# One last fold in one VectorE operation, and a new order of statements on four engines

## The chip, the cores and the metric

The kernel runs on one core of a Trainium2 chip. The metric is the device time of one execution in microseconds (us). Below, "the profile" is one execution recorded by the hardware profiler. Engines: TensorE (PE, its weight loads PEld), VectorE (DVE), ScalarE (ACT), GpSimd (POOL), SyncE (SP).

## The reference, cut to what matters

```
for l in range(2):                                   # L0, a graph network, two layers
    m_left, m_right = h @ W_left[l].T, h @ W_right[l].T
    u = h @ m_left.T / temper   (upper triangle and diagonal), h @ m_right.T / temper   (lower)
    e = exp(u) * adj
    h = relu(layer_norm((e / (sum(e) + 1e-10)) @ (h @ W_lin[l].T + b_lin[l])))
x = layernorm(x + h)
q, k, v = x @ Wq.T, x @ Wk.T, x @ Wv.T + bv           # L1, attention, 12 heads of 32
scores = q @ k.T * scale + (adj + adj)
row_nonzero = any(scores != 0, axis=-1)
p = nan_to_num(softmax(where(row_nonzero, scores, -inf)))
x = layernorm(x + (p @ v) @ Wo.T + bo)
```

There are 128 graphs of 128 nodes with 384 features. A row whose scores are all zero ("dead") must give zero. The kernel decides that from the row's maximum and from the sum of its scores.

## The kernel before, in words

The 128 graphs are worked in 32 groups of four. One *pass* (`body(p)` on each engine) does L0 of group `it` and L1 of group `it - 1`; what L1 does for its last graph (`pv`, `to`, `po` with b = 3) comes at the start of the next pass. Pass 0 (which also rounds the weights, `setup`), pass 1 and the last passes 32 and 33 leave parts out. Products are made from float16 pairs: a high part rounded by ScalarE, a low part (the difference) by VectorE or GpSimd, three matmuls for each product.

Each engine has its own written-out list of statements; they meet through semaphores. TensorE's statements of one pass: `nl(l, c)` six products of layer l with W_left and W_right, nine matmuls of 512 columns each; `hl(l, b)` the linear part of graph b, nine of 384; `u(l, h)` scores of two graphs, 18 of 256; `ctx(l, b)` the context, three of 386; `th(k)` and `x1t(k)` four transposes each; `qk(c)` six, nine matmuls of 512 each; `v(b)` nine of 384; `scores(b, c)` 12 small groups on 32 rows; `pt(b, r)` four transposes of the softmax weights; `pv(b)` 36 matmuls of 33 columns; `to(b)` three transposes of the attention output `o`; `po(b)` nine of 384.

VectorE reads most results out of PSUM: `nl`, `qk`, `pt`, `x1t`, `to` form low parts; `scores(b, j)` subtracts the adjacency and takes the row's extreme (`nmax`); `rs_of(b)` is a reciprocal and a multiplication by the mask `live`; `pv(b)` scales to `o`; `den`, `bn`, `z_variance`, `inv_std(0)`, `norm_z` are the layer norm of L0's first layer, after which TensorE transposes `z` in `th`; `po_stats` and `fin` are the last layer norm. ScalarE does the exponentials (`exps`, `exp_u`), the rounding and `fin`. GpSimd does low parts (`hl`, `v`, `xt`), the masks, powers and the folds.

The eight PSUM banks have a written-out order of use, `BANK_USES`. A stage that gets a bank waits (`await_bank`) until the stage that had it before has been read, by the signal in `READ`.

The dead-row sum: for each graph b, `folds(b)` on GpSimd adds halves of the 12 x 128 scores, 64 + 64, 32 + 32, ... in six folds in the tile `fold`, and a seventh addition writes `total` (12 numbers), signal `s_tot`. VectorE's `live_of(b)` waits for `s_tot` and makes `live`. `scores(b)` for b >= 2 waits for `fold1` of b - 2 before it overwrites `s`.

Of the kernel before, what the change touches and what calls it, by code (L numbers as in the profile page):

```python
# [5 lines left out]
GROUP = 4  # L6
# [24 lines left out]
def program(nc, x, xT, adj, adjT, weights, biases, ln_cols, ln_rows, out):  # L31
# [5 lines left out]
    with ExitStack() as stack:  # L37
# [62 lines left out]
        def signal(name, per_group):  # L100
# [12 lines left out]
            for p in ("u_full", "u_read", "u_sum", "e_raw", "e_ok", "e_hi_ok", "e_lo_ok"))  # L113
# [16 lines left out]
        fold1, fold2, fold3, fold4, fold5, fold6, s_tot = (  # L130
            signal(p, GROUP) for p in ("fold1", "fold2", "fold3", "fold4", "fold5", "fold6", "s_tot"))
# [15 lines left out]
                     s_full, s_ok, s_tot, fold1, fold2, fold3, fold4, fold5, fold6, p_ok, pt_full, pt_hi, pt_lo, pv_full, live_ok, rcp_ok,  # L147
# [9 lines left out]
        def uses(*runs):  # L157
# [29 lines left out]
        class Pass:  # L187
# [40 lines left out]
            def await_bank(self, eng, stage, *parts):  # L228

                last = {}  # L230
# [101 lines left out]
        def _(pool):  # L332
# [148 lines left out]
            def body(p):  # L481
# [3 lines left out]
                hl(p, 0, 1)  # L485
                out_bias(p, 0)
                weigh(p, 0, 0)
                e_rest(p, 0, 0)
                weigh(p, 0, 1)
                hl(p, 0, 2)  # L490
                e_rest(p, 0, 1)
                out_bias(p, 1)
                hl(p, 0, 3)
                out_bias(p, 2)
                y2_power(p, 3)
                scale_adj(p)
                z_power(p, 0)
                out_bias(p, 3)
                v(p, 0)
                folds(p, 0)  # L500
                folds(p, 1)
                v(p, 1)
                xt(p, 0)
# [12 lines left out]
                hl(p, 1, 2)
                hl(p, 1, 3)
                xt(p, 2)
                y2_power(p, 1)
                mask_left(p)  # L520
                mask_right(p)
                y2_power(p, 2)
# [11 lines left out]
        def _(act):  # L534
# [142 lines left out]
            def body(p):  # L677
                nl(p, 0, 0)
                setup(p, 2)
                setup(p, 3)  # L680
                setup(p, 4)
                nl(p, 0, 1)
# [4 lines left out]
                nl(p, 0, 5)  # L687
                x1_norm(p, 2)
                x1_norm(p, 3)
                hl(p, 0, 0)  # L690
# [3 lines left out]
                x1t(p, 1)  # L694
                x1t(p, 2)
                round_e(p, 0, 0)
                exp_u(p, 0, 1)
                fin(p, 2)
                hl(p, 0, 2)
                qk(p, 0)  # L700
                round_e(p, 0, 1)
                hl(p, 0, 3)
                ctx(p, 0, 0)
                qk(p, 1)
                ctx(p, 0, 1)
# [5 lines left out]
                setup(p, 5)  # L711
                qk(p, 5)
                setup(p, 6)
                v(p, 0)
                th(p, 0)
                th(p, 1)
                exps(p, 0, 0)
                exps(p, 0, 1)
                exps(p, 0, 2)
                th(p, 2)  # L720
                exps(p, 0, 3)
                exps(p, 1, 0)
                pt(p, 0, 0)
                exps(p, 1, 1)
# [3 lines left out]
                pt(p, 1, 0)  # L728
                setup(p, 7)
                nl(p, 1, 1)  # L730
                xt(p, 0)
                exps(p, 1, 2)
                nl(p, 1, 2)
                setup(p, 8)
                setup(p, 9)
                v(p, 1)
                fin(p, 3)
                v(p, 2)
                nl(p, 1, 3)
                to(p, 0)  # L740
# [8 lines left out]
                exps(p, 2, 2)  # L749
                hl(p, 1, 0)  # L750
                exps(p, 2, 3)
                pt(p, 2, 0)
                to(p, 1)
                pt(p, 2, 1)
                pt(p, 2, 2)
                exps(p, 3, 0)
                exps(p, 3, 1)
                exps(p, 3, 2)
                exps(p, 3, 3)
                hl(p, 1, 1)  # L760
                v(p, 3)
                fin(p, 0)
                exp_u(p, 1, 0)
                xt(p, 2)
                pt(p, 3, 0)
                round_e(p, 1, 0)
                to(p, 2)
                exp_u(p, 1, 1)
                hl(p, 1, 2)
                round_e(p, 1, 1)  # L770
                pt(p, 3, 1)
                pt(p, 3, 2)
# [17 lines left out]
        def _(dve):  # L790
# [293 lines left out]
            def body(p):  # L1084
# [3 lines left out]
                scale_z(p, 1)  # L1088
                nl(p, 0, 0)
                pv(p, 3)  # L1090
                nl(p, 0, 1)
                scale_z(p, 2)
                scale_z(p, 3)
                inv_std(p, 1)
                to(p, 3)
                shift_z(p, 0)
                shift_z(p, 1)
                shift_z(p, 2)
                shift_z(p, 3)
                nl(p, 0, 2)  # L1100
                resid(p, 0)
                resid(p, 1)
                po(p, 3)
                y_bn(p, 0)
                y_bn(p, 1)
                setup(p, 2)
                setup(p, 3)
                setup(p, 4)
                nl(p, 0, 3)
                resid(p, 2)  # L1110
                resid(p, 3)
                nl(p, 0, 4)
                nl(p, 0, 5)
                y_bn(p, 2)
                y_bn(p, 3)
                y_variance(p)
                hl(p, 0, 0)
                resid_inv(p)
                resid_norm(p, 0)
                hl(p, 0, 1)  # L1120
                resid_norm(p, 1)
                u(p, 0, 0)
                fin(p, 2)
                u_add(p, 0, 0)
# [4 lines left out]
                x1t(p, 2)  # L1129
                hl(p, 0, 2)  # L1130
                hl(p, 0, 3)
                po_stats(p, 3)
                den(p, 0, 0)
                qk(p, 0)
                bn(p, 0, 0)
                bn(p, 0, 1)
                qk(p, 1)
                den(p, 0, 1)
                bn(p, 0, 2)
                bn(p, 0, 3)  # L1140
# [9 lines left out]
                norm_z(p, 3)  # L1150
                qk(p, 5)
                v(p, 0)
                setup(p, 5)
# [4 lines left out]
                th(p, 0)  # L1158
# [3 lines left out]
                th(p, 1)  # L1162
                scores(p, 1, 0)
                th(p, 2)
                scores(p, 1, 1)
                setup(p, 6)
                scores(p, 1, 2)
                pt(p, 0, 0)
                setup(p, 7)
                scores(p, 1, 3)  # L1170
                pt(p, 0, 1)
                pt(p, 0, 2)
                nl(p, 1, 0)
                live_of(p, 0)
# [373 lines left out]
```

## Time and profile before

| | |
|---|---|
| median of 3 runs | 2868.6 us (2867.44 to 2870.93) |
| profiled execution, device time | 2869.89 us |
| its span | 2868.0 us |
| mean granted TensorE clock | 0.992 |
| busy: TensorE | 2794.6 us (97%) |
| busy: VectorE | 2406.5 us (84%) |
| busy: ScalarE | 1770.5 us (62%) |
| busy: GpSimd | 1657.6 us (58%) |

The span goes from the first to the last instruction; the device time has 1.9 us more around it. TensorE is nearly always busy, so what is to be read is where it is not.

### The profile page before, as it was taken

The page shows a single profiled execution, that of the slowest core. Times are in us where ns is not written, and L with a number is a line of the kernel's source. Part 1 is how long each engine was busy: PE and PEld are TensorE (multiplying, and loading weights), DVE is VectorE, ACT ScalarE, POOL GpSimd, SP SyncE. Part 2 cuts the span into 40 slices and gives each one's busy share as a digit, 9 for nine tenths or more (in the row PEclk, how much of TensorE's full clock was granted, in tenths as well). Part 3 has the DMA queues.
Part 4 walks back from the last instruction along what each step waited for, and adds up shares of the span by engine and source line. Part 5 has one row for each costly group of instructions (what it writes and reads, how often), then busy time and mean ns, then how long its engine had stood idle before and what let it go on. Part 6 is the DMA issues. An engine that isn't in the chain of part 4 may idle for free.

```text
span 2868.0 us, 69803 instructions
## 1 busy us (share of the span) xinstructions
PE 2794.6 (97%) x24768; PEld 1790.0 (62%) x24768; DVE 2406.5 (84%) x8042; ACT 1770.5 (62%) x4107; POOL 1657.6 (58%) x2097
## 2 busy tenths in 40 slices
PE   7999999999999999999999999999999999999996
PEld 4566666666665666666666656666666666566664
DVE  5788888888888888888888888888888888888886
ACT  4556666556665556665566655566655666555664
POOL 2556565556565565655565655656555656555554
PEclk9999999999999999999999999999999999999998
DMA  4001011111011010111010110101110101101000
GB/s 151 30 32 45 21 46 40 41 36 34 32 43 43 32 45 21 45 40 44 33 35 31 43 43 31 45 21 45 40 45 32 41 25 43 43 32 45 21 27 21
DMA packets 55976, 112.21 MB, mean 39 GB/s; under 512 B 4944, under 2 KB 37712, under 8 KB 55632
## 3 DMA queue, kind: packets, MB, share of 16 engines
q1 hardware_dynamic: 55632, 107.76, 11.0%
q8 instruction: 199, 3.26, 0.5%
q14 instruction: 145, 1.19, 0.1%
HBM read 82.58 MB, written 25.17 MB: 38 GB/s over the span
## 4 chain that ended last, share of the span: by engine, by line
PE 86%; DVE 10%; ACT 2%; issue 1%; POOL 0%; DMA 0%; DVEq 0%; SPq 0%; POOLq 0%; ACTq 0%
PE psum L1250 62%; PE psum L1260 11%; PE psum L1311 9%; PE psum L1404 3%; PE psum L1378 2%; DVE z L1016 2%; DVE nT_lo L813 2%; DVE pT_lo L811 1%; DVE rs L876 1%; DVE qk_lo L813 1%; ACT qk_hi L536 1%; ACT pT_hi L536 1%; DVE st L915 1%; DVE o L888 1%; DVE y L907 1%
## 5 line engine op out<-in xcount | busy, mean ns | idle before, releaser
L596 ACT ACTIVATE w<-s,nmax 128x128 f32<-128x128 f32 x1536 | 479.4, 403 | 1.9 <-DVE nmax L846 1.9
L1250 PE MATMUL psum<-hT_hi,w_hi 128*128 128x512 f16 x1152 | 439.1, 381 | 13.3 <-POOL hT_lo L379 11.9
L1250 PE MATMUL psum<-hT_lo,w_hi 128*128 128x512 f16 x1152 | 438.7, 381 | 0.0
L1250 PE MATMUL psum<-hT_hi,w_lo 128*128 128x512 f16 x1152 | 438.4, 381 | 0.0
L536 ACT ACTIVATE nT_hi<-psum 128x512 f16<-128x512 f32 x384 | 230.1, 599 | 271.0 <-PE psum L1250 270.9
L463 POOL TENSOR_TENSOR fold<-fold 128x384 f32<-128x384 f32 (+4 forms) x640 | 342.8, 536 | 50.1
L846 DVE CUSTOM_DVE_ANT_0 s<-psum,adj 128x128 f32<-128x128 f32 x1536 | 341.0, 284 | 30.8 <-PE psum L1378 30.0
L463 POOL TENSOR_TENSOR fold<-s 128x768 f32<-128x768 f32 x128 | 242.3, 1893 | 193.5 <-DVE nmax L846 193.5
L387 POOL TENSOR_TENSOR hl_lo<-hl_raw,hl_hi 128x384 fp32r<-128x384 f32 x256 | 245.3, 963 | 147.5 <-ACT hl_hi L536 143.6
L811 DVE TENSOR_TENSOR pT_lo<-psum,pT_hi 128x512 f16<-128x512 f32 x384 | 253.2, 683 | 37.7 <-ACT pT_hi L536 37.5
L536 ACT ACTIVATE pT_hi<-psum 128x512 f16<-128x512 f32 x384 | 222.0, 598 | 85.3 <-PE psum L1260 85.1
L813 DVE SCALAR_TENSOR_TENSOR nT_lo<-psum,nT_hi 128x512 f16<-128x512 f32 x384 | 256.1, 681 | 11.9 <-ACT nT_hi L536 11.7
L430 POOL TENSOR_TENSOR yrstd<-yvar,pw 128x4 f32<-128x4 f32 x32 | 32.4, 1012 | 403.7 <-DVE yvar L996 403.7
L536 ACT ACTIVATE z<-psum,rden 128x384 f32<-128x384 f32 x256 | 138.1, 578 | 182.4 <-DVE rden L962 182.4
L1250 PE MATMUL psum<-w_hi,hT_lo 128*128 128x384 f16 x768 | 250.4, 326 | 0.0
L1250 PE MATMUL psum<-w_lo,hT_hi 128*128 128x384 f16 x768 | 250.4, 326 | 0.0
L1250 PE MATMUL psum<-w_hi,hT_hi 128*128 128x384 f16 x768 | 250.4, 326 | 0.0
L1250 PE MATMUL psum<-xT_hi,w_hi 128*128 128x512 f16 x576 | 219.6, 381 | 0.0
L1250 PE MATMUL psum<-xT_lo,w_hi 128*128 128x512 f16 x576 | 218.7, 380 | 0.0
L1250 PE MATMUL psum<-xT_hi,w_lo 128*128 128x512 f16 x576 | 218.6, 380 | 0.0
L1260 PE MATMUL psum<-ident,w 128*128 128x128 f32 x1536 | 207.4, 275 | 2.6 <-DVE nmax L846 2.2
L1311 PE MATMUL psum<-nT_hi,hT_lo 128*128 128x256 f16 x768 | 209.3, 273 | 0.0
(133 smaller groups left out, 7948.5 us busy)
## 6 DMA issues: line engine op xcount, KB each, us to landing
xTin<-xT SPq DMA_DIRECT2D x32, 768.0 KB, 4.7
xres<-x SPq DMA_DIRECT2D x32, 768.0 KB, 4.6
out<-y SPq DMA_DIRECT2D x128, 192.0 KB, 1.9
adjn<-adj SPq DMA_DIRECT2D x32, 256.0 KB, 4.9
adjT_sb<-adjT SPq DMA_DIRECT2D x32, 256.0 KB, 5.0
adj<-adj SPq DMA_DIRECT2D x32, 256.0 KB, 2.8
x<-weights SPq DMA_DIRECT2D x4, 576.0 KB, 5.4
s<-weights SPq DMA_DIRECT2D x3, 576.0 KB, 6.4
```

The source lines that it names most:

```text
L387: nc.gpsimd.tensor_tensor(hl_lo[:, b, 0:FEAT], hl_raw[:, b], hl_hi[:, b, 0:FEAT].bitcast(f32), ALU.subtract).then_inc(hlr_lo[l].sem, 1)
L463: nc.gpsimd.tensor_tensor(fold[:, :, 0:n], src[:, :, 0:n], src[:, :, n:2 * n], ALU.add)\
L536: return nc.scalar.activation(dst, src, ACT.Copy, scale=scale)
L596: last = nc.scalar.activation(w[:, m], s[b % 2][:, m], ACT.Exp, bias=nmax[b % 2][:, m:m + 1], scale=-1.0)
L811: nc.vector.tensor_tensor(dst, src, rounded, ALU.subtract).then_inc(done.sem, 1)
L813: nc.vector.scalar_tensor_tensor(dst, src, scale, rounded, ALU.mult, ALU.subtract)\
L846: last = nc.vector.tensor_tensor_reduce(out=s[b % 2][:, m], in0=psum[:, SC[j], c * TOK:(c + 1) * TOK], in1=adj2[:, b], scale=-1.0 / TEMPER ...
L1016: nc.vector.tensor_scalar(z[:, b], z[:, b], rstd[0][:, b:b + 1], nmr[:, b:b + 1], ALU.mult, ALU.add)\
L1250: last = mm(dst, a, b, start=(i == 0), stop=(i == total - 1))
L1260: last = transpose(dst[:, n * 128:(n + 1) * 128], src, ident[:])
L1311: last = mm(dst, a, m, start=(i == 0), stop=(i == len(terms) - 1))
L1404: last = mm(dst[:, n * VCOL:(n + 1) * VCOL], a, m, start=(i == 0), stop=(i == 2))
```

## The change

Three things. GpSimd stops after the third fold (16 numbers left for each of 12 heads); `live_of(b)` on VectorE waits for `fold3` and sums the 16 in one `tensor_reduce` into `total`, then makes `live` as before. With that, GpSimd's `folds(b + 1)` waits for VectorE's `s_tot` of b. All four engines' lists of statements stand in another order, and the banks are used in another order. And in `scores` the wait for `qk` of the first graph is merged with the bank's (`also`), so that the later of the two stands. SyncE's statements stay.

```diff
-                for n, src_ok, done in ((TOK // 2, None, fold1), (TOK // 4, fold1, fold2), (TOK // 8, fold2, fold3),
-                                        (TOK // 16, fold3, fold4), (TOK // 32, fold4, fold5),
-                                        (TOK // 64, fold5, fold6)):
+                for n, src_ok, done in ((TOK // 2, None, fold1), (TOK // 4, fold1, fold2), (TOK // 8, fold2, fold3)):
...
-                pool.wait_ge(fold6.sem, p.upto(fold6, b + 1))
-                if b >= 2:
-                    pool.wait_ge(live_ok.sem, p.upto(live_ok, b - 1))
-                elif p.before.l1:
-                    pool.wait_ge(live_ok.sem, p.before.upto(live_ok, b + 3))
-                nc.gpsimd.tensor_tensor(total[b % 2][:], fold[:, :, 0], fold[:, :, 1], ALU.add)\
-                    .then_inc(s_tot.sem, 1)
...
 def live_of(p, b):                                   (VectorE)
+                dve.wait_ge(fold3.sem, p.upto(fold3, b + 1))
+                nc.vector.tensor_reduce(total[b % 2][:], fold[:, :, 0:TOK // 8], AX.X, ALU.add).then_inc(s_tot.sem, 1)
                 dve.wait_ge(s_tot.sem, p.upto(s_tot, b + 1))
...
 def scores(p, b, c):                                 (TensorE)
-                    p.await_bank(pe, "s", *range(TILES * b, TILES * (b + 1)))
-                if b == 0:
+                    p.await_bank(pe, "s", *range(TILES * b, TILES * (b + 1)), also=(("qk", 1),) if b == 0 else ())
+                elif b == 0:
                     pe.wait_ge(qkr_lo.sem, p.upto(qkr_lo, 2 * c + 2))
```

TensorE's order, before and after, from the middle of a pass on (`s` is all three blocks of `scores`):

```
before: qk0 qk1 ctx0,0 ctx0,1 qk2 ctx0,2 ctx0,3 qk3 qk4 qk5 v0 th0 s0 th1 v1 v2 v3 th2 s1 pt0,0 pt0,1 nl1,0 nl1,1 pt0,2 pt1,0 nl1,2 pv0 nl1,3 s2 to0 nl1,4 pt1,1 pt1,2 po0 nl1,5 pv1 hl1,0 s3 to1 hl1,1 pt2,0 pt2,1 pt2,2 u1,0 po1 pv2 u1,1 pt3,0 to2 hl1,2 pt3,1 hl1,3 pt3,2 po2 ctx1,0..3
after:  qk0 ctx0,0 ctx0,1 qk1 ctx0,2 ctx0,3 qk2 qk3 qk4 qk5 th0 th1 v0 s0(0,1) th2 s0(2) v1 v2 v3 s1 pt0,0 pt0,1 nl1,0 pt0,2 nl1,1 pv0 nl1,2 s2 to0 nl1,3 pt1,0 pt1,1 pt1,2 nl1,4 po0 nl1,5 pv1 pt2,0 s3 hl1,0 pt2,1 u1,0 hl1,1 pt2,2 hl1,2 pt3,0 to1 pt3,1 pv2 u1,1 pt3,2 hl1,3 to2 po1 po2 ctx1,0..3
```

VectorE's order around the two places that the prediction speaks of:

```
before: ... den0,1 bn bn z_variance0 qk2 qk3 qk4 fin3 inv_std0 norm_z(4) qk5 v0 scores0 th0 ...
after:  ... den0,1 bn bn bn z_variance0 qk1 qk2 fin3 inv_std0 norm_z(4) qk3 qk4 qk5 th0 v0 th1 scores0 ...
before: ... scores1,1 scores1,2 pt0,0 scores1,3 pt0,1 pt0,2 nl1,0 live0 pt1,0 rs0 nl1,1 pv0 nl1,2 scores2 ... nl1,3 po0 po_stats0 nl1,4 nl1,5 live1 rs1 pv1 hl1,0 scores3 to1 ...
after:  ... scores1,1 pt0,0..2 scores1,2 live0 rs0 scores1,3 pv0 nl1,0 nl1,1 scores2,0..2 to0 scores2,3 nl1,2 pt1,0..2 live1 po0 nl1,3 nl1,4 po_stats0 rs1 nl1,5 pt2,0 pv1 hl1,0 scores3,0..2 u1,0 scores3,3 live2 hl1,1 pt2,1 pt2,2 u_add1,0 to1 rs2 ...
end, before: ... po2 live3 den1,0 po_stats2 den1,1 bn(4) fin1;  after: ... po1 pt3,2 po2 po_stats1 den1,0 po_stats2 den1,1 bn(4) fin1
start, before: ... resid0 resid1 po3 y_bn0 ...;  after: ... resid0 resid1 y_bn0 y_bn1 scale_z3 nl0,3..5 po3 ...
```

GpSimd: `z_power(0)` and `scale_adj` now come ahead of `y2_power(3)` and of two of the four `out_bias`; `v`, `xt` come earlier, the two `folds` of graphs 2 and 3 after them. ScalarE: `th(2)` ahead of all `exps`, `fin(3)` ahead of `pt(0,0)`, and in pass 0 the weight roundings 5 and 6 ahead of `ctx(0,0)`.

## Rows read from the trace of the kernel before

**Rows 1.** Stretches: one steady pass, and the last 88 us (busy time, number of instructions).

```profile
core 0: us, PE busy (x) PEld busy (x) DVE busy (x) ACT busy (x) POOL busy (x), PEclk, DMA share, GB/s
...
1087.52:1175.10 87.58, 86.73 (x775) 55.76 (x774) 74.78 (x252) 54.84 (x129) 51.77 (x65) 1.00 0.12 38
...
2780.00:2868.00 88.00, 59.74 (x584) 37.38 (x582) 60.97 (x224) 41.86 (x100) 37.19 (x53) 0.82 0.06 22
```

**Rows 2.** TensorE's waits from 120 to 2690 us: total, times, longest.

```profile
PE psum L1260 <- DVE o L888: 16.3, 28, 0.6
PE psum L1260 <- DVE z L1016: 7.2, 29, 0.3
```

**Rows 3.** TensorE's timeline around `to(0)`, `to(1)`, `th(0)`: start, us, operation, [idle before].

```profile
1096.17 0.23 PE L1378 MATMUL psum<-qk_hi,qk_lo 32*128 32x128 f16 x4
1096.33 0.55 PE L1260 MATMUL psum<-ident,o 128*128 128x128 f32 x3
...
1105.86 0.22 PE L1378 MATMUL psum<-qk_hi,qk_lo 32*128 32x128 f16 x4
1106.68 0.55 PE L1260 MATMUL psum<-ident,o 128*128 128x128 f32 x3 [0.60 <-DVE o L888]
...
1164.87 0.33 PE L1250 MATMUL psum<-w_hi,xT_lo 128*128 128x384 f16 x1
1165.44 0.66 PE L1260 MATMUL psum<-ident,z 128*128 128x128 f32 x4 [0.25 <-DVE z L1016]
```

**Rows 4.** The chain of waits where the transposes of `x1` start, passes 1 and 31.

```profile
95.48 1.31 PE psum L1260 x12
...
2721.96 1.31 PE psum L1260 x12
```

**Rows 5.** VectorE's timeline: `rs_of(1)`, the last `nmax` of graph 3, L0's layer norm.

```profile
1104.92 1.04 DVE L876 SCALAR_TENSOR_TENSOR rs<-live,rs 128x12 f32<-128x12 f32 x1
...
1109.54 0.08 DVE L846 DVE_READ_ACCUMULATOR2_ANT nmax<- 128x1 f32 x1
...
1158.00 0.15 DVE L959 TENSOR_SCALAR eps_den<-psum 128x2 f32<-128x2 f32 x1
1158.18 0.17 DVE L962 RECIPROCAL rden<-eps_den 128x2 f32<-128x2 f32 x1
...
1160.40 0.17 DVE L986 TENSOR_SCALAR var<-mv 128x4 f32<-128x4 f32 x1
...
1162.45 0.69 DVE L813 SCALAR_TENSOR_TENSOR qk_lo<-psum,qk_hi 128x512 f16<-128x512 f32 x1 [0.69 <-ACT qk_hi L536]
...
1163.74 1.65 DVE L1016 TENSOR_SCALAR z<-z,rstd,nmr 128x384 f32<-128x384 f32 x4
```

**Rows 6.** GpSimd's timeline at the same places.

```profile
1104.78 1.15 POOL L379 TENSOR_TENSOR hT_lo<-xTin,hT_hi 128x512 f16<-128x512 f32 x1
...
1109.76 1.81 POOL L463 TENSOR_TENSOR fold<-s 128x768 f32<-128x768 f32 x1 [0.52 <-DVE nmax L846]
...
1156.94 0.62 POOL L445 TENSOR_SCALAR adj<-adj 128x512 f32<-128x512 f32 x1
1160.66 1.02 POOL L430 TENSOR_TENSOR sd<-var,pw 128x4 f32<-128x4 f32 x1 [3.10 <-DVE var L986]
```

**Rows 7.** The chain of waits: `pt`, `scores`, `nl`, `hl`, `u` on TensorE, start to start.

```profile
1084.11 0.44 PE psum L1260 x4
1084.54 0.61 PE psum L1378 x36
...
1093.83 1.95 PE psum L1250 x9
...
1107.23 1.46 PE psum L1250 x9
...
1110.00 1.96 PE psum L1311 x18
```

**Rows 8.** GpSimd's groups: the first and the last of the four operations removed.

```profile
L463 POOL TENSOR_TENSOR fold<-fold 128x96 f32<-128x96 f32 x128 | 50.0, 391 | 10.0
...
L471 POOL TENSOR_TENSOR total<-fold 128x12 f32<-128x12 f32 x128 | 27.4, 214 | 10.1
```

More of the change, by code:

```diff
@@ L129, in program @@
         s_full, s_ok, p_ok = (signal(p, GROUP * TILES) for p in ("s_full", "s_ok", "p_ok"))
-        fold1, fold2, fold3, fold4, fold5, fold6, s_tot = (
-            signal(p, GROUP) for p in ("fold1", "fold2", "fold3", "fold4", "fold5", "fold6", "s_tot"))
+        fold1, fold2, fold3, s_tot = (signal(p, GROUP) for p in ("fold1", "fold2", "fold3", "s_tot"))
         pt_full, pt_hi, pt_lo = (signal(f"pt_{p}", GROUP * KB) for p in ("full", "hi", "lo"))
@@ L226, in await_apart, with await_bank @@
                 eng.wait_ge(sig.sem, value)
-            def await_bank(self, eng, stage, *parts):
-                last = {}
+            def await_bank(self, eng, stage, *parts, also=()):
+                last = {name: (self.group(READ[name]), i) for name, i in also}
                 for i in parts:
@@ L485, in body @@
                 hl(p, 0, 1)
-                out_bias(p, 0)
[L487 to L491, printed above, removed]
+                weigh(p, 0, 0)
+                weigh(p, 0, 1)
+                e_rest(p, 0, 0)
+                e_rest(p, 0, 1)
+                hl(p, 0, 2)
+                hl(p, 0, 3)
+                out_bias(p, 0)
                 out_bias(p, 1)
-                hl(p, 0, 3)
-                out_bias(p, 2)
-                y2_power(p, 3)
                 scale_adj(p)
                 z_power(p, 0)
+                y2_power(p, 3)
+                v(p, 0)
+                out_bias(p, 2)
                 out_bias(p, 3)
-                v(p, 0)
                 folds(p, 0)
@@ L727, in body @@
                 nl(p, 1, 0)
-                pt(p, 1, 0)
-                setup(p, 7)
+                exps(p, 1, 0)
                 nl(p, 1, 1)
-                xt(p, 0)
+                exps(p, 1, 1)
                 exps(p, 1, 2)
[L733 to L740, printed above, removed]
                 exps(p, 1, 3)
                 xt(p, 1)
+                to(p, 0)
+                xt(p, 2)
+                v(p, 1)
+                setup(p, 8)
+                v(p, 2)
+                nl(p, 1, 2)
+                v(p, 3)
+                setup(p, 9)
+                pt(p, 1, 0)
+                nl(p, 1, 3)
                 pt(p, 1, 1)
@@ L1087, in body @@
                 scale_z(p, 0)
-                scale_z(p, 1)
                 nl(p, 0, 0)
                 pv(p, 3)
+                scale_z(p, 1)
                 nl(p, 0, 1)
+                inv_std(p, 1)
                 scale_z(p, 2)
-                scale_z(p, 3)
[L1094 to L1097, printed above, removed]
+                to(p, 3)
+                nl(p, 0, 2)
+                shift_z(p, 0)
+                setup(p, 2)
+                shift_z(p, 1)
+                resid(p, 0)
+                resid(p, 1)
+                y_bn(p, 0)
+                setup(p, 3)
+                y_bn(p, 1)
+                scale_z(p, 3)
+                nl(p, 0, 3)
+                nl(p, 0, 4)
+                nl(p, 0, 5)
+                setup(p, 4)
+                po(p, 3)
                 shift_z(p, 2)
                 shift_z(p, 3)
[L1100 to L1109, printed above, removed]
                 resid(p, 2)
                 resid(p, 3)
-                nl(p, 0, 4)
-                nl(p, 0, 5)
                 y_bn(p, 2)
@@ L1116, in body @@
                 y_variance(p)
+                u(p, 0, 0)
                 hl(p, 0, 0)
                 resid_inv(p)
+                u_add(p, 0, 0)
                 resid_norm(p, 0)
+                resid_norm(p, 1)
                 hl(p, 0, 1)
[L1121 to L1124, printed above, removed]
                 u(p, 0, 1)
@@ L1129, in body @@
                 x1t(p, 2)
+                fin(p, 2)
                 hl(p, 0, 2)
                 hl(p, 0, 3)
-                po_stats(p, 3)
                 den(p, 0, 0)
                 qk(p, 0)
+                po_stats(p, 3)
                 bn(p, 0, 0)
+                den(p, 0, 1)
                 bn(p, 0, 1)
-                qk(p, 1)
-                den(p, 0, 1)
                 bn(p, 0, 2)
@@ L1150, in body @@
                 norm_z(p, 3)
+                setup(p, 5)
+                qk(p, 3)
+                qk(p, 4)
                 qk(p, 5)
+                setup(p, 6)
+                th(p, 0)
                 v(p, 0)
-                setup(p, 5)
+                th(p, 1)
                 scores(p, 0, 0)
@@ L1161, in body @@
                 v(p, 3)
-                th(p, 1)
+                th(p, 2)
                 scores(p, 1, 0)
-                th(p, 2)
                 scores(p, 1, 1)
-                setup(p, 6)
-                scores(p, 1, 2)
                 pt(p, 0, 0)
-                setup(p, 7)
-                scores(p, 1, 3)
                 pt(p, 0, 1)
                 pt(p, 0, 2)
+                scores(p, 1, 2)
+                live_of(p, 0)
+                setup(p, 7)
+                rs_of(p, 0)
+                scores(p, 1, 3)
+                pv(p, 0)
                 nl(p, 1, 0)
-                live_of(p, 0)
-                pt(p, 1, 0)
-                rs_of(p, 0)
                 nl(p, 1, 1)
-                pv(p, 0)
-                nl(p, 1, 2)
+                setup(p, 8)
                 scores(p, 2, 0)
                 scores(p, 2, 1)
+                scores(p, 2, 2)
                 to(p, 0)
-                setup(p, 8)
-                scores(p, 2, 2)
                 scores(p, 2, 3)
+                nl(p, 1, 2)
+                pt(p, 1, 0)
                 pt(p, 1, 1)
                 pt(p, 1, 2)
+                live_of(p, 1)
+                po(p, 0)
                 nl(p, 1, 3)
-                po(p, 0)
+                nl(p, 1, 4)
                 po_stats(p, 0)
-                nl(p, 1, 4)
+                rs_of(p, 1)
                 nl(p, 1, 5)
-                live_of(p, 1)
-                rs_of(p, 1)
+                pt(p, 2, 0)
                 pv(p, 1)
-                setup(p, 9)
                 hl(p, 1, 0)
@@ L1200, in body @@
                 scores(p, 3, 2)
+                u(p, 1, 0)
+                setup(p, 9)
                 scores(p, 3, 3)
-                to(p, 1)
+                live_of(p, 2)
                 hl(p, 1, 1)
-                pt(p, 2, 0)
                 pt(p, 2, 1)
                 pt(p, 2, 2)
-                u(p, 1, 0)
-                po(p, 1)
                 u_add(p, 1, 0)
+                to(p, 1)
+                rs_of(p, 2)
                 fin(p, 0)
-                live_of(p, 2)
-                rs_of(p, 2)
+                hl(p, 1, 2)
                 pv(p, 2)
-                po_stats(p, 1)
+                live_of(p, 3)
                 u(p, 1, 1)
                 u_add(p, 1, 1)
-                to(p, 2)
-                hl(p, 1, 2)
                 pt(p, 3, 0)
                 hl(p, 1, 3)
+                to(p, 2)
                 pt(p, 3, 1)
+                po(p, 1)
                 pt(p, 3, 2)
                 po(p, 2)
-                live_of(p, 3)
+                po_stats(p, 1)
                 den(p, 1, 0)
@@ L1479, in body @@
                 to(p, 0)
[L1480 removed]
+                nl(p, 1, 3)
+                pt(p, 1, 0)
                 pt(p, 1, 1)
                 pt(p, 1, 2)
+                nl(p, 1, 4)
                 po(p, 0)
```

139 lines of the change are left out of this document (67 added, 72 removed).

## The prediction

> **What bounds the kernel now.** I read the stretches first, then TensorE's waits, then the chain of waits, then the timelines of the two places that they name. One steady pass takes 87.58 us and TensorE is busy for 86.73 of them [rows 1]. So a schedule can give back 0.85 us of a pass, about 1%, unless it makes the matmuls themselves cheaper, and this change alters none. The other engines have room: VectorE 12.8 us, ScalarE 32.7, GpSimd 35.8 in the same pass. They matter only where TensorE waits for them. Between 120 and 2690 us only two waits of TensorE are left [rows 2]: `to(p, 1)`, the transpose of `o`, 28 times, 16.3 us, and `th(p, 0)`, the transpose of the normalised `z`, 29 times, 7.2 us. Together 23.5 us in 29 passes, 0.81 each.
>
> Idle time is a little less than what is lost, since the last matmul's record runs on after the next could have started. From start to start [rows 3]: before `to(0)`, which does not wait, the last scores matmul and the transpose are 0.16 us apart (1096.17, 1096.33); before `to(1)` 0.82 us (1105.86, 1106.68). Lost: 0.66 us. Before `th(0)` 0.57 us (1164.87, 1165.44), where matmuls of this width follow at 0.16: 0.41 us. The true loss is 1.07 us a pass.
>
> How often: the transposes of `x1` start at 95.48 us in pass 1 and at 2721.96 us in pass 31 [rows 4], 2626.5 us in 30 steps, 87.55 each. With pass 31's second half that is 31 passes.
>
> **Why the two waits exist.** `to(1)`: `pv(1)` ends on TensorE, VectorE forms `rs` and `o`, and TensorE has only `hl(1,0)` and `scores(3)` in between, 1.46 + 0.76 us. The second operation of `rs_of` took 1.04 us instead of 0.17 (the row at 1104.92), and ended when GpSimd's `xt` of 1104.78 to 1105.93 ended [rows 5, 6]. So the two engines block each other there. `th(0)`: from the end of `ctx(0,3)` VectorE works through `den` (1158.00), `bn`, `z_variance` (ends at 1160.57, 2.6 us later), then three `qk` subtractions, of which the last waits 0.69 us for ScalarE, and only then the normalisation, 1.65 us, from 1163.74 to 1165.39 [rows 5]. TensorE reaches `th(0)` after three `qk` and one `v`, 3 x 1.95 + 1.46 = 7.3 us [rows 7], just too early.
>
> **The change, part by part.** *Fold.* GpSimd loses four operations for each of four graphs, each 0.21 to 0.39 us [rows 8]: 0.9 to 1.6 us a graph, 3.4 to 6.3 us a pass, from an engine that idles 35.8. Nothing on TensorE waited for it directly: 0. VectorE gains one `tensor_reduce` of 192 numbers into 12. The trace has none. Below, it costs what a tiny operation does, 0.17 us (the reciprocal at 1158.18); above, what reading 512 numbers does, 0.69 us (1162.45) [rows 5]. Its width of 192 puts it a third of the way: I take 0.35. Four times that, plus a hand-over of 0.03 us each (1158.15 to 1158.18), is 1.5 us a pass (0.8 to 2.9). VectorE has 12.8 us free and it lies under TensorE's work: 0, if no consumer stands close behind. Where the cover is gone it costs its own 0.35 us, once for each such place.
>
> *`to(1)`.* TensorE now does `pt(2,0)`, `scores(3)`, `hl(1,0)`, `pt(2,1)`, `u(1,0)`, `hl(1,1)`, `pt(2,2)`, `hl(1,2)`, `pt(3,0)` between `pv(1)` and `to(1)`: 4 x 0.44 + 0.76 + 3 x 1.46 + 1.96 = 8.9 us [rows 7]. VectorE needs `rs_of` 0.35 (1.2 if blocked), `nl`, `pt`, `pv`, together 2.1 to 3 us. The wait goes: -0.66.
>
> *`th(0)`.* From the end of `ctx(0,3)`: `den`, two copies of `z`, the last `bn`, `z_variance` to 2.5 us; GpSimd's power 1.02 [rows 6], and now `y2_power(3)` behind it, at most as much again, since `fin(3)` stands before `inv_std` on VectorE; 4.7 us at worst; `inv_std` 0.5; normalisation 1.65: 6.9 us. `qk(3)` and `qk(4)` are now behind it. TensorE arrives after four `qk`, 7.8 us. Slack 0.9: -0.41.
>
> *What it adds on TensorE.* `th(2)` is now put between the second and third block of `scores(0)`. A turn from transposes to the 32-row matmuls or back costs about 0.1 us more than a step without a turn (0.16 at 1096.17 to 1096.33, against 0.07, which is 0.61 us over the nine steps of four matmuls in `scores`) [rows 3, 7]. One split adds two turns: +0.2, bounds 0 and 0.4.
>
> *What is late next.* I laid every engine's statements end to end from these prices and looked at each bank and each operand. The tightest places are: `scores(2,0)` needs its bank read by `scores(1,3)`, now behind `rs_of(0)`, which waits for `pv(0)`: 0.35 + 0.64 + 0.1 = 1.1 us against TensorE's `nl(1,2)`, 1.95: slack 0.85. `to(0)`: 1.7 us against 2.7: 1.0. `pv(1)` uses the bank that `nl(1,3)` leaves; from the end of `po(0)`, VectorE reads both in 1.15, TensorE has `nl(1,5)`, 1.95: 0.8. `u(1,0)` uses the bank of `pv(1)`; from its end TensorE has two `pt`, `scores(3)` and `hl(1,0)`, 3.1, VectorE `rs_of`, `nl`, `pt`, `pv`, 2.2: 0.9. `to(2)`, `po(1)`, `po(2)` now stand in a row: ScalarE 0.5 and VectorE 0.55 against 1.46: 0.4. `ctx(1,2)` uses the bank of `po(2)`, two contexts after it, six matmuls at 0.16 to 0.18, against one read of 0.55: 0.5. None is negative, so 0 for each; they are thin.
>
> *The hold on `fold`.* `folds(b+1)` now waits for VectorE's `live_of(b)`. For b = 1 the fold of graph 2 starts some 3 us after its scores are ready. `scores(b)` on VectorE waits for the first fold of graph b-2 only: 0. The queue of SyncE: its statements stay, and the load of `adj2` stands behind `store(2)`, hence behind `fin(2)`, which keeps its place between `x1t` and `hl(0,2)`. `scale_adj`, which found its data ready (no idle time at 1156.94), comes an `out_bias` and a power earlier, 1.6 us. Even if it waited all of that, `z_power(0)` behind it idles 3.10 us for VectorE [rows 6]: 0.
>
> *Head and tail.* Pass 0 keeps its serial chain; two weight roundings of ScalarE come ahead of the first `ctx` copies: +0.5, bounds -1 and +2. In the last 88 us TensorE is busy for 59.7 [rows 1]: here the chain of single operations sets the time. `po_stats(1)` is later, `po(3)` behind two more statistics: +1.5, bounds -3 and +5.
>
> **The sum.** 31 x (-0.66 - 0.41 + 0.2) = -27.0; head and tail +2.0; -25.0. The profiled execution took 2869.9 us (span 2868.0, and 1.9 around it), 1.3 above the median of the runs, so 2844.9 in its terms and 2843.6 in the median's: 2844.
>
> **The rivals.**
> *A (0.62)*: as summed, 2834 to 2850. The low end is a split that costs nothing (31 x 1.07 = 33) and a tail that gains 1.5.
> *B, thin slots (0.18)*: one or two of the slots of 0.4 to 0.9 us fail in part. A blocked VectorE operation is late by up to 0.9 us (1.04 against 0.17); `rs_of(1)` now falls into the last folds of graph 2, say. If one such hits a slot of 0.4, TensorE waits 0.5: 31 x (0.87 - 0.5) = 11 us gain, 2859 with the tail. Range 2850 to 2863.
> *C, no difference (0.09)*: what the two waits hid comes back at two slots, 0.7 to 1.0 us a pass: 2863 to 2874. For it: my slots are sums of ten prices and each could be off by that much; against it: all would have to err to one side, and each leaves 0.4 or more.
> *D, the lock race, slower (0.11)*: the reduce's signal releases two things at once: VectorE's own `live` operation and GpSimd's first fold of the next graph, 1.81 us [rows 6]. If the fold goes first, `live` is blocked as `rs` was at 1104.92, and VectorE stands still for 1.8 us, for b = 1 and b = 2, where the scores are already there. Then `nl(1,3)` frees its bank 1.75 late with a slack of 0.8: wait 0.95; and `pt(2,2)`/`hl(1,1)` are late by 1.75 with slacks of 1.2: wait 0.6. Net -0.87 + 1.55 = +0.68 a pass, +21 us: 2891. With one place alone it is +0.1 a pass, rival C. It decides from a stall of about 1.4 us on. Against it: VectorE follows its own signal by 0.03 us, while GpSimd started 0.14 us after `nmax` (1109.62, 1109.76) [rows 5, 6].
>
> The Trainium skill, "SBUF — State Buffer", section on practical consequences, says that a VectorE instruction with two SBUF inputs and a GpSimd instruction that reads SBUF block each other fully and that the first to issue wins; the 1.04 us row agrees. It also says that `tensor_reduce` never contends on this chip, which no run here shows yet. By this rule only `live` and `rs` are exposed, not the reduce. That is the mechanism of D.
>
> **The numbers.** A and B are faster: 0.80. C: 0.09. D: 0.11. A measurement of this kernel tells about 0.2% (5.7 us) from no change. The range that keeps 8 in 10: 2834 to 2864, A and B with their bounds.
>
> **What the changed profile would show.** Right: a steady pass of 86.7 us; the waits for `o` and `z` gone from TensorE's list between 120 and 2690 us; no new row there above 5 us; `total` on VectorE at 0.3 to 0.4 us; `live` with a median near 0.16 us. Wrong: `live` with a median of a microsecond (D); a new wait of TensorE for `oT_lo`, `nmax` or `nT_lo` (B, C); a tail longer than 93 us. I am wrong above all if a slot that I give 0.4 to 0.9 us is in truth shut.

## The result and the profile after

The changed kernel takes 2845.7 us (median of 4 runs, 2845.1 to 2847.13); the kernel before, beside it, 2868.0. Ratio 0.9921 with a 95% interval of 0.9904 to 0.9938: 22 us or 0.8% faster. The forecast was 2844 us, with a range of 2834 to 2864.

The steady pass of the changed kernel, and its last 85 us, by stretches. They answer to [rows 1]:

```profile
1051.27:1137.92 86.65, 86.65 (x777) 55.85 (x775) 76.18 (x256) 55.42 (x128) 46.75 (x50) 1.00 0.11 38
...
2759.00:2844.20 85.20, 55.18 (x549) 35.40 (x546) 58.29 (x223) 38.58 (x91) 28.26 (x31) 0.80 0.06 20
```

A pass takes 86.65 us and TensorE is busy in all of it. VectorE works 1.4 us more, GpSimd 5.0 us less. From 120 to 2690 us the list of TensorE's waits is empty; where [rows 2] had 23.5 us there is no line. The list of its weight loads has only these (total, times, longest). No idle time of the matmuls goes with them, which alone does not prove that they cost nothing (see e8):

```profile
PEld psum L1371 <- issue: 41.3, 148, 0.4
PEld psum L1243 <- issue: 14.5, 88, 0.2
PEld psum L1243 <- DVE oT_lo L802: 4.7, 30, 0.2
PEld psum L1253 <- DVE pT_lo L802: 0.4, 1, 0.4
```

The chain of waits, at the transposes of `x1` in passes 1 and 31 (compare [rows 4]):

```profile
98.14 1.50 PE psum L1253 x12
...
2697.57 1.31 PE psum L1253 x12
```

2599.4 us in 30 passes, 86.65 each, against 87.55: 0.90 us less. Up to the first of the two the new kernel is 1.2 us slower (2.66 us later, of which 1.46 are `hl(0,2)`, which now comes ahead of `x1t`). The 30 passes give -27.0. From the second to the end, with the same correction, it is 2.05 us slower. 1.2 - 27.0 + 2.05 is -23.8 us, the difference of the two spans (2868.0 and 2844.2).

The two operations of `live_of`, from the tiles `total` and `live` of the changed kernel (min/median/max in ns):

```profile
L855 DVE TENSOR_REDUCE total<-fold x128: 333/343/349, 129.0 to 2826.0; 128x12 f32<-128x192 f32 x128
L857 DVE SCALAR_TENSOR_TENSOR live<-nmax,total x128: 170/171/173, 129.4 to 2826.4; 128x12 f32<-128x12 f32 x128
```

### The profile page after: what moved, and what is told of

Read it like the earlier page. It is cut to its first block, busy times and chain, and to the rows that moved or that the text cites. A ratio compares the mean times of both kernels' runs of the same rounds, so it can differ in the third digit from the quotient of the medians.

```text
span 2844.2 us, 69230 instructions
## 1 busy us (share of the span) xinstructions
PE 2792.3 (98%) x24768; PEld 1793.3 (63%) x24768; DVE 2447.5 (86%) x8170; ACT 1784.8 (63%) x4107; POOL 1497.1 (53%) x1585
## 4 chain that ended last, share of the span: by engine, by line
PE 97%; DVE 1%; issue 1%; ACT 1%; DMA 0%; POOL 0%; SPq 0%; POOLq 0%; DVEq 0%; ACTq 0%
PE psum L1243 70%; PE psum L1253 11%; PE psum L1304 9%; PE psum L1397 4%; PE psum L1371 3%; DMA xTin<-xT 0%; DMA s<-weights 0%; ACT w L587 0%; ACT w_hi L527 0%; DVE st L962 0%; POOL hl_lo L387 0%; DVE w_lo L785 0%; DVE st L908 0%; POOL e L416 0%; DVE y L900 0%
## 5 line engine op out<-in xcount | busy, mean ns | idle before, releaser
L461 POOL TENSOR_TENSOR fold<-s 128x768 f32<-128x768 f32 x128 | 232.7, 1818 | 224.5 <-DVE nmax L837 139.6
L527 ACT ACTIVATE hl_hi<-hl_raw 128x384 fp32r<-128x384 f32 x256 | 133.1, 520 | 300.5 <-DVE hl_raw L817 300.5
L387 POOL TENSOR_TENSOR hl_lo<-hl_raw,hl_hi 128x384 fp32r<-128x384 f32 x256 | 252.6, 993 | 125.7 <-ACT hl_hi L527 125.6
L395 POOL TENSOR_TENSOR v_lo<-v_raw,v_hi 128x384 f16<-128x384 f32 x128 | 112.5, 890 | 283.1 <-ACT v_hi L527 283.1
L461 POOL TENSOR_TENSOR fold<-fold 128x384 f32<-128x384 f32 (+1 forms) x256 | 217.8, 851 | 20.0
L1253 PE MATMUL psum<-ident,w 128*128 128x128 f32 x1536 | 220.1, 277 | 4.0 <-DVE nmax L837 2.0
```

Source lines behind the costliest of these rows:

```text
L387: nc.gpsimd.tensor_tensor(hl_lo[:, b, 0:FEAT], hl_raw[:, b], hl_hi[:, b, 0:FEAT].bitcast(f32), ALU.subtract).then_inc(hlr_lo[l].sem, 1)
L395: nc.gpsimd.tensor_tensor(v_lo[:, b, :, 0:HEAD], v_raw[:, b].rearrange("p (h d) -> p h d", h=HEADS), v_hi[:, b, :, 0:HEAD], ALU.subtract). ...
L527: return nc.scalar.activation(dst, src, ACT.Copy, scale=scale)
L1253: last = transpose(dst[:, n * 128:(n + 1) * 128], src, ident[:])
```

## The experiments

Each run was timed beside the kernel before. "A pass" is the distance between the transposes of `x1` in pass 1 and pass 31 divided by 30; it is 87.55 us in the kernel before.

| run | median us | ratio to before, 95% interval | a pass, us |
|---|---|---|---|
| e1 fold only | 2970.4 | 1.0354 (1.0340 to 1.0369) | 90.61 |
| e2 order only | 2845.2 | 0.9919 (0.9905 to 0.9932) | 86.61 |
| e3 `norm_z` first | 2878.2 | 1.0033 (1.0020 to 1.0045) | 87.82 |
| e4 `to(1)` later | 2868.2 | 0.9999 (0.9990 to 1.0008) | 87.51 |
| e5 e3 and `out_bias(3)` later | 2855.7 | 0.9954 (0.9941 to 0.9966) | 87.10 |
| e6 e4 and two banks exchanged | 2850.4 | 0.9936 (0.9924 to 0.9949) | 86.92 |
| e7 e5 and e6 together | 2834.7 | 0.9881 (0.9866 to 0.9896) | 86.43 |
| e8 changed, `th(2)` whole | 2843.9 | 0.9913 (0.9900 to 0.9927) | 86.57 |
| e9 e1 with a tile of its own | 2862.9 | 0.9979 (0.9970 to 0.9988) | 87.29 |
| e10 changed, three reduces | 2866.6 | 0.9994 (0.9985 to 1.0003) | 87.25 |
| e11 changed, `out_bias` early | 2863.1 | 0.9981 (0.9973 to 0.9990) | 87.20 |
| e12 changed, five reduces | 2874.2 | 1.0018 (1.0009 to 1.0027) | 87.44 |

### Which part brings the gain: the fold alone (e1), the order alone (e2)

e1 is the kernel before with the three edits of the fold (signals, `folds`, `live_of`) and no other line changed.

> The order of before, with the fold's change alone. My theory (the order brings the gain, the fold gives none by itself): in the old order the reduce stands in live_of(1), right ahead of rs_of(1), pv(1) and to(1), where TensorE already waits, so its 0.34 us and a hand-over come on top of the wait, unless GpSimd's shorter folds take away the blocked rs operation (1.04 instead of 0.17 us). I expect 2868 + 31 x 0.38 = 2880 us, and at least 2863. Rival (the fold is the gain): 2845 to 2855 us, with TensorE's waits for o and z smaller.

e2 is the changed kernel with the old `folds` and `live_of`:

```diff
-                for n, src_ok, done in ((TOK // 2, None, fold1), (TOK // 4, fold1, fold2), (TOK // 8, fold2, fold3)):
+                for n, src_ok, done in ((TOK // 2, None, fold1), (TOK // 4, fold1, fold2), (TOK // 8, fold2, fold3),
+                                        (TOK // 16, fold3, fold4), (TOK // 32, fold4, fold5),
+                                        (TOK // 64, fold5, fold6)):
...
-                nc.vector.tensor_reduce(total[b % 2][:], fold[:, :, 0:TOK // 8], AX.X, ALU.add).then_inc(s_tot.sem, 1)
```

> The order and banks of after, with GpSimd doing all seven additions as before. My theory: 2843 to 2850 us, TensorE without waits in the middle, VectorE 48 us less busy than in after; in the new order live_of(0) comes 0.4 us after the old, longer folds would be done, so at most 0.3 us a pass is lost there. Rival (the new order works only because GpSimd has 6 us less to do): a new wait behind live_of, 2855 to 2870 us.

e2 took 2845.2 us: the order and the banks are the whole gain, the fold adds nothing to it. e1 took 2970.4 us. The sign was right and the size wrong by eight times: 102 us lost, not 12. e2's time lies in its forecast. The waits of GpSimd in e1, from 120 to 2690 us:

```profile
POOL fold L460 <- DVE total L854: 488.4, 87, 6.6
POOL yrstd L429 <- DVE yvar L988: 347.7, 28, 12.6
```

In the old order `live_of` stands late on VectorE, which cost nothing as long as GpSimd did not need it. Now GpSimd's next fold waits for it, 5.6 us at a time, and with the fold everything queued behind it: `hl`, `weigh`, `e_rest`. And the fold that starts on VectorE's signal blocks an operation on two SBUF tiles that VectorE issues just behind it. VectorE's timeline in e1, and GpSimd's below it:

```profile
1047.81 0.17 DVE L856 SCALAR_TENSOR_TENSOR live<-nmax,total 128x12 f32<-128x12 f32 x1
...
1048.16 1.53 DVE L868 SCALAR_TENSOR_TENSOR rs<-live,rs 128x12 f32<-128x12 f32 x1
...
1047.86 1.80 POOL L460 TENSOR_TENSOR fold<-s 128x768 f32<-128x768 f32 x1 [5.72 <-DVE total L854]
```

`live` is issued 0.05 us before the fold and passes; `rs`, behind it, ends at 1049.69, just after the fold (1049.66). This is the rule in e1, not the exception; the 128 second operations of `rs_of` (min/median/max in ns) in e1, and below in e9, the next run:

```profile
L868 DVE SCALAR_TENSOR_TENSOR rs<-live,rs x128: 170/941/1544, 131.0 to 2957.1; 128x12 f32<-128x12 f32 x128
...
L874 DVE SCALAR_TENSOR_TENSOR rs<-live,rs x128: 170/172/875, 132.0 to 2850.5; 128x12 f32<-128x12 f32 x128
```

### What of e1's loss is the hold (e9)

The third fold writes a small tile of its own, `last`, two of them in turn, so GpSimd's next fold no longer waits for VectorE's sum:

```diff
+        last = [sb(f"last{i}", [HEADS, TOK // 8]) for i in range(2)]
...
                 if b > 0:
-                    pool.wait_ge(s_tot.sem, p.upto(s_tot, b))
+                    pool.wait_ge(fold3.sem, p.upto(fold3, b))
...
+                    if done is fold3 and b > 1:
+                        pool.wait_ge(s_tot.sem, p.upto(s_tot, b - 1))
...
+                nc.vector.tensor_reduce(total[b % 2][:], last[b % 2][:, :, 0:TOK // 8], AX.X, ALU.add).then_inc(s_tot.sem, 1)
```

> The fold's change alone in the order of before, as in the first run, but the third fold writes a small tile of its own, two of them in turn, so that GpSimd's next fold waits for its own third fold and no longer for VectorE's reduce. Theory (the hold on the tile cost the 102 us: GpSimd waited 488 us for total there, and hl_lo and weigh behind it came late): the time falls from 2970 us to 2868 + 31 x 0.38 = 2880 us, 2865 to 2890. Rival (the reduce, and rs blocked by GpSimd's folds, cost it): it stays above 2930 us.

2862.9 us: with the hold go all 102 us of the loss and 5.4 more, so the fold's change by itself is a gain even in the old order, where I had expected a loss (2880, at least 2865). The 107 us between e1 and e9 have two parts that this run takes away together, GpSimd's wait for `total` and most of the blocking of `rs`; how they share it was not tested. In its trace the idle time for `o` is down to this:

```profile
PE psum L1258 <- DVE z L1014: 7.2, 29, 0.2
PE psum L1258 <- DVE o L886: 0.5, 2, 0.2
```

GpSimd is earlier and no longer in the middle of an operation when `rs_of(1)` comes: in the pass read, its `xt` ends at 1015.16, and `rs` starts at 1016.00 and takes 0.17 us. That this is why the wait shrinks was not tested by itself. And it is not gone: from start to start, in the mean of 25 passes, the step before `to(1)` is 0.44 us shorter than in the kernel before, not 0.66, and `pt(3,0)` and `to(2)` take 0.24 us more than there, with next to no idle time in the list for either.

### The wait for `z` alone (e3, e5)

```diff
                 qk(p, 2)
-                qk(p, 3)
-                qk(p, 4)
                 fin(p, 3)
                 inv_std(p, 0)
                 norm_z(p, 0)
...
                 norm_z(p, 3)
+                qk(p, 3)
+                qk(p, 4)
                 qk(p, 5)
```

> The order of before with one move on VectorE: fin(3), inv_std(0) and the four norm_z ahead of qk(3) and qk(4). My theory: the wait for z is a matter of this place alone and is worth 0.41 us a pass: 2868 - 31 x 0.41 = 2855 us, if qk(3), qk(4) and qk(5), now later, still come in time for scores(0); TensorE's wait for o stays. Rival: the wait moves on to the scores or to th(1), 2866 to 2870 us.

It was 10 us slower. TensorE's wait for `z` is gone from the list, and in its place stand 9.7 us of waiting for `qk_lo` (29 times). VectorE's and GpSimd's timelines in e3:

```profile
1077.35 0.96 DVE L1003 TENSOR_SCALAR sd_eps<-sd 128x4 f32<-128x4 f32 x1 [0.48 <-POOL sd L430]
...
1077.28 1.00 POOL L405 TENSOR_TENSOR x<-x,bias 128x384 f32<-128x384 f32 x1
```

`sd_eps` now comes right after GpSimd's power, and so does GpSimd's next statement, `out_bias(3)`, 0.07 us earlier. It takes 0.96 us for a four-column operation. It has one SBUF input, so it is not only operations with two that are blocked. e5 adds one exchange on GpSimd:

```diff
                 z_power(p, 0)
-                out_bias(p, 3)
                 v(p, 0)
+                out_bias(p, 3)
```

> The third run's move (fin(3), inv_std(0), norm_z ahead of qk(3) and qk(4) on VectorE) and, with it, GpSimd's out_bias(3) behind v(0) instead of right behind z_power(0). Theory: in the third run VectorE's first operation after the power, sd_eps, was blocked by out_bias(3) for 0.97 instead of 0.17 us in every pass; with GpSimd idle there it is not, and the time falls by 31 x 0.8 = 25 us from 2878 us to about 2855 us. Rival: the late qk subtractions are the cause (TensorE waits for qk_lo), the blocked operation is not, 2872 to 2880 us.

2855.7 us, with `sd_eps` never above 0.171 us and the wait for `qk_lo` gone as well. The wait for `z` is worth 0.45 us a pass (forecast 0.41), but it needs two engines' orders, not one. The changed kernel has both edits.

### The wait for `o` alone (e4, e6)

TensorE's list (VectorE's likewise):

```diff
                 scores(p, 3, 2)
-                to(p, 1)
                 hl(p, 1, 1)
+                to(p, 1)
```

> The order of before with to(1) moved behind hl(1,1) on TensorE and on VectorE. My theory: 1.46 us of matmuls now cover the 0.66 us that are lost: 2868 - 31 x 0.66 = 2847.5 us, TensorE's wait for o gone, its wait for z as before. Rival: VectorE's chain is the bound there and TensorE waits for pt(2,*) or po(1) instead, 2860 to 2870 us.

No change at all. TensorE's timeline in e4:

```profile
1017.16 0.22 PE L1378 MATMUL psum<-qk_hi,qk_lo 32*128 32x128 f16 x4
1017.99 0.34 PE L1250 MATMUL psum<-w_hi,hT_hi 128*128 128x384 f16 x1 [0.60 <-DVE o L888]
```

`hl(1,1)` now has the very wait that `to(1)` had. It does not read `o`; it writes into the bank out of which VectorE forms `o`. The old order had two reasons to wait at the same place, and the profile names only the first that comes. e6:

```diff
-            ... ("nl1", 4), ("to", 1), ("pv", 2), ("c1", 0)),
+            ... ("nl1", 4), ("hl1", 1), ("pv", 2), ("c1", 0)),
...
-                 ("po", 0), ("pv", 1), ("hl1", 1), ("po", 1), ("pt", 10)),
+                 ("po", 0), ("pv", 1), ("to", 1), ("po", 1), ("pt", 10)),
```

> The fourth run's move (to(1) behind hl(1,1)) and, with it, their two PSUM banks exchanged: hl(1,1) takes the bank that nl(1,4) leaves, to(1) the one that pv(1) leaves. Theory: in the fourth run hl(1,1) waited for the same VectorE operation as to(1) had, because its bank is the one out of which o is formed; with another bank the 0.66 us a pass are covered by its 1.46 us: 2868.5 - 31 x 0.66 = 2848 us, TensorE's wait for o gone. Rival: VectorE's chain behind it (pt, u, po) is as late, 2860 to 2869 us.

2850.4 us, 0.63 us a pass (forecast 0.66). So this half of the gain comes from the new `BANK_USES` as much as from the new order.

### Both, and nothing else (e7)

> The two runs above in one kernel: order of before, four local edits, no change of the fold. Theory: the two waits are independent, 2868.5 - 31 x 1.07 = 2835 us, TensorE without waits in the middle, less than the new order's 2845.7 since scores(0) is not split and head and tail are those of before. Rival: removing one lets the other grow, 2845 to 2855 us.

2834.7 us: the waits add up, 1.12 us a pass (0.45 and 0.63 alone), and this kernel, the one before with four local edits, beats the changed one by 11 us. Its pass takes 86.43 us:

```profile
1000.00:1086.43 86.43, 86.43 (x776) 55.98 (x775) 74.87 (x252) 55.01 (x129) 52.18 (x66) 1.00 0.11 38
```

Between the two spans (2833.5 and 2844.2) lie 10.7 us: 6.4 in the 30 passes, 2.8 ahead of the first of them and 1.5 behind the last, with `hl(0,2)` counted as above.

### The split of `scores(0)` (e8)

```diff
                 scores(p, 0, 1)
-                th(p, 2)
                 scores(p, 0, 2)
+                th(p, 2)
                 v(p, 1)
```

> The changed kernel with th(2) behind scores(0,2) instead of between scores(0,1) and scores(0,2) on TensorE. Theory: two turns between transposes and 32-row matmuls fall away, 0.2 us a pass: 2845.7 - 6 = 2839.5 us, a steady pass of 86.45 us. Rival: the turns cost nothing or th(2) is then late for nl(1,0), 2845 to 2847 us.

The chain of waits, from the first block of `scores(0)` to the end of `v(3)`, first in the changed kernel:

```profile
1070.20 0.45 PE psum L1371 x24
1070.64 0.59 PE psum L1253 x4
1071.23 0.28 PE psum L1371 x12
1071.51 4.49 PE psum L1243 x27
```

and in e8:

```profile
1069.58 0.61 PE psum L1371 x36
1070.19 0.59 PE psum L1253 x4
1070.78 4.39 PE psum L1243 x27
```

5.81 against 5.59 us: the two turns cost 0.22 us, as estimated. But the pass is only 0.08 us shorter and the kernel 1.8 us faster, between the forecast and its rival. The rest shows in the chain: `pv(0)` takes 0.99 us instead of 0.90, and `nl(1,0)` and `pt(0,2)` ahead of it 0.02 more each, 0.13 in all. TensorE has no idle time there. But the list of its weight loads, from 120 to 2690 us, has three waits that the changed kernel's has not:

```profile
PEld psum L1397 <- issue: 11.7, 30, 0.4
PEld psum L1243 <- DVE hT_lo L1030: 10.1, 30, 0.3
PEld psum L1253 <- DVE nmax L837: 9.1, 30, 0.3
```

`hT_lo` is what VectorE makes of `th`, so the rival (`th(2)` late for `nl(1,0)`) came in part. That these waits cause the 0.13 us fits by place and was not tested.

### How wide the slots are (e10, e12, e11)

e10 and e12 put two and four more reduces ahead of the real one:

```diff
+                for i in range(2):
+                    nc.vector.tensor_reduce(spare_out[i][:], fold[:, :, 0:TOK // 8], AX.X, ALU.add).then_inc(spare, 1)
                 nc.vector.tensor_reduce(total[b % 2][:], fold[:, :, 0:TOK // 8], AX.X, ALU.add).then_inc(s_tot.sem, 1)
```

> The changed kernel with the reduce done three times (twice into unused tiles, ahead of the real one), +0.55 to 0.7 us on VectorE for each graph. Theory (slots of 0.8 us behind live_of(1), 1.1 behind live_of(2), 0.4 left at po(2) behind live_of(3)): the slots take it, 0 to 0.2 us a pass, 2846 to 2852 us. Rival (the slots are nearly shut): 31 x 4 x 0.6, up to 2920 us, with new waits of TensorE.

> As the run with three reduces, with five, +1.1 to 1.4 us on VectorE for each graph, 4.4 to 5.6 us a pass. Theory: now the slots are overrun: about 0.5 us at pv(1), 0.2 at pv(2) and pt(3,0), 0.5 at po(2), together 0.5 to 1.2 us a pass: 2861 to 2883 us. Rival (VectorE has 12 us free, it is hidden): 2846 to 2850 us.

e10 took 2866.6 us, more than the theory had and much less than the rival: 0.60 us a pass. TensorE waits at one place only, `po(2)`. VectorE in e10, then GpSimd, then TensorE:

```profile
1028.93 0.60 DVE L858 TENSOR_REDUCE spare_out<-fold 128x12 f32<-128x192 f32 x2
...
1030.63 0.95 DVE L946 TENSOR_TENSOR e<-uLR 128x256 f32<-128x256 f32 x1
...
1032.56 0.54 DVE L804 TENSOR_TENSOR oT_lo<-psum,oT_hi 128x384 f16<-128x384 f32 x1
...
1030.57 0.73 POOL L428 TENSOR_TENSOR e_lo<-e,e_hi 128x256 fp32r<-128x256 f32 x1 [1.68 <-ACT e_hi L529]
...
1033.16 0.34 PE L1247 MATMUL psum<-w_hi,oT_hi 128*128 128x384 f16 x1 [0.54 <-DVE oT_lo L804]
```

The two reduces before `live_of(3)` cost 0.52 us. They push `u_add(1,1)` behind the start of GpSimd's `e_rest`, and it takes 0.95 instead of 0.43 us. In the changed kernel it gets ahead:

```profile
1108.87 0.43 DVE L942 TENSOR_TENSOR e<-uLR 128x256 f32<-128x256 f32 x1
...
1109.32 0.73 POOL L426 TENSOR_TENSOR e_lo<-e,e_hi 128x256 fp32r<-128x256 f32 x1 [1.75 <-ACT e_hi L527]
...
1110.78 0.56 DVE L802 TENSOR_TENSOR oT_lo<-psum,oT_hi 128x384 f16<-128x384 f32 x1 [0.35 <-ACT oT_hi L527]
...
1111.46 0.33 PE L1243 MATMUL psum<-w_hi,oT_hi 128*128 128x384 f16 x1
```

Here `oT_lo` ends at 1111.34, 0.12 us before `po(2)` starts, not 0.4. e12, with twice the load, lost 0.80 us a pass, inside its forecast. TensorE's idle time does not show where: from 120 to 2670 us it is 6.0 us, in 29 passes that lost 23. The steps from start to start do. In the mean of 25 passes, against the changed kernel, `po(1)` and `po(2)` take 0.36 us more, `hl(1,2)` 0.19, `nl(1,2)` 0.12, and the `pt` of graphs 2 and 3 together 0.13. The chain of waits behind `hl(1,2)`, in the changed kernel and then in e12:

```profile
1017.23 1.20 PE psum L1253 x11
...
1025.86 0.03 issue
1025.89 1.42 PE psum L1257 x11
```

So with 1 us more in front of each `live` several slots are overrun, each by less than the load.

e11 exchanges GpSimd's `v(0)` with `out_bias(2)` and `out_bias(3)` in the changed kernel.

> The changed kernel with out_bias(2) and out_bias(3) of GpSimd ahead of v(0) again, right behind z_power(0) and y2_power(3). Theory: they block sd_eps and the nmr behind it, as out_bias(3) did in the third run, 0.8 us each; the slot in front of th(0) is 0.9 to 1.3 us, so TensorE waits 0.3 to 0.7 us a pass: 2855 to 2868 us, sd_eps with a median above 0.7 us. Rival: the blocked operations fit into the slot, 2845 to 2848 us, with the same sd_eps.

2863.1 us, as forecast, 0.55 us a pass. The operations blocked were others than I had named. `sd_eps` passed between the two biases; those hit are the two with two inputs, in `fin(3)` and in `inv_std(0)`. VectorE's timeline in e11, and the row of GpSimd's two biases below it:

```profile
1073.24 0.95 DVE L923 SCALAR_TENSOR_TENSOR nmr<-mv,rstd 128x1 f32<-128x1 f32 x1 [0.47 <-POOL rstd L430]
1074.12 0.16 DVE L996 TENSOR_SCALAR sd_eps<-sd 128x4 f32<-128x4 f32 x1
...
1074.52 0.63 DVE L1001 SCALAR_TENSOR_TENSOR nmr<-mv,rstd 128x4 f32<-128x4 f32 x1
...
1073.18 1.95 POOL L405 TENSOR_TENSOR x<-x,bias 128x384 f32<-128x384 f32 x2
```

Without the biases both take 0.16 us. Where two statements of GpSimd stand is worth 17 us.

## Why the prediction was right, point by point

**What bounds the kernel.** Right. Loss counted from start to start, 1.07 us a pass, not the 0.81 us of idle time: e7 shows that 1.12 us can be had.

**`to(1)`, -0.66.** Right in size, incomplete in cause. The prediction named only the operand `o`. e4 and e6 show a second wait on the same operation, for the bank. I counted a gain for the new place of `to(1)`; it needed the new banks too, and these were in the change.

**`th(0)`, -0.41.** Right in size (0.45 in e5; the prediction counted up to the first transpose, and the four of `th(0)` are 0.06 us shorter in e5 as well). In the changed kernel `z` is ready at 1066.70 and `th(0)` starts at 1067.70: slack 1.0 us, forecast 0.9. The `fin(3)` in front of `inv_std` waits 0.47 us for its power, as expected. What the prediction left out is why GpSimd's biases moved: e3 and e11 show that they would have taken the slot.

**The fold.** The reduce costs 0.343 us; I took 0.35. Its effect on the time was put at 0 and is 0 in the new order (e2: 2845.2 against 2845.7). The prediction's part on the hold was right for the new order (there GpSimd waits for `total` 77 us from 120 to 2690, and TensorE waits for nothing) but would have been wrong by some 100 us for the old one (e1, e9). Cover was a matter of the order, not of the operation.

**The split, +0.2.** The turns cost 0.22 us (e8). With the 1.12 us that the two waits give back (e7) this makes -0.90 a pass, which is what was measured; the forecast was -0.87. Undoing the split in the new order gives back only 0.08 us a pass.

**What is late next.** No slot was overrun. `po(2)` was named as the tightest, at 0.4 us; it has 0.12. Two reduces more ahead of each `live` are enough to overrun it, by 0.60 us a pass (e10).

**Head and tail, +2.0.** Mis-sized: 1.2 us at the head and, with the last pass's gain of 0.9 taken out, 2.9 at the tail, 4.1 together. The passes made good 0.9 of the 2.1 us: 31 x 0.90 is 27.9 instead of 27.0. What in the head and the tail cost it was not tested.

**The rivals.** B and C did not come. D, the lock race, did not come either: the longest `live` of 128 took 0.173 us. It goes 0.05 us before the fold (1102.15 and 1102.20 in VectorE's and GpSimd's timelines), as the prediction argued. Its mechanism is real one operation later: in the old order `rs` stands there (e1). In the new order `rs_of` is never directly behind `live_of(1)` or `live_of(2)`; its second operation is still blocked in 63 of 128 cases by other work of GpSimd (0.96 us instead of 0.17 at worst), but TensorE waits for none of them. Nor is `live` safe everywhere: in e1, 30 of its 128 take 1.2 us, those of graph 3. The Trainium skill's rule, "SBUF — State Buffer", practical consequences, that the first to issue wins for the whole instruction, agrees with these rows. Its statement that `tensor_reduce` never contends agrees too. In the changed kernel no reduce begins while GpSimd is in an operation, so that kernel is no test. In e1 31 do, and in e9 61, and none of them takes over 0.345 us. VectorE in e1, and GpSimd's row below it (two operations, the second from about 1068.3 to 1069.2):

```profile
1068.78 0.34 DVE L854 TENSOR_REDUCE total<-fold 128x12 f32<-128x192 f32 x1
1069.15 1.18 DVE L856 SCALAR_TENSOR_TENSOR live<-nmax,total 128x12 f32<-128x12 f32 x1
...
1067.35 1.84 POOL L386 TENSOR_TENSOR hl_lo<-hl_raw,hl_hi 128x384 fp32r<-128x384 f32 x2
1069.15 1.16 POOL L378 TENSOR_TENSOR hT_lo<-xTin,hT_hi 128x512 f16<-128x512 f32 x1
```

## What to carry to other kernels

TensorE's idle time can be far less than what a wait costs: in e12 it was 6 us where 23 were lost. So count from start to start, against the same place in a kernel without the wait. A wait in the profile names one reason; before moving the waiting statement, look whether the one that takes its place waits for the same thing through its buffer. On VectorE and GpSimd read the two timelines side by side: who is issued first behind a shared signal decides about a microsecond, on statements that seem to have nothing to do with each other. And a new order that removes all waits need not be the best: four local edits, each made for one wait, gave half as much again as the rewritten order.

## What was not expected of the hardware

An operation of VectorE with a single SBUF input and four columns (`sd_eps`, a `tensor_scalar`) took 0.96 us instead of 0.17 while GpSimd added 384 columns (e3). `out_bias(3)` had started 0.07 us before. The same operation passed in 0.16 us in e11, where it was issued 0.01 us before the second of two such additions; in 1 of 64 cases there it took 0.97 us too.
